# Turned attention probabilities moved to their key partitions through device memory: one store and four loads per unit in place of sixteen transfers inside SBUF

## The reference, cut to what matters

```python
x = x + attn(_layernorm(x))            # 32 query heads, 8 key-value heads, head width 128
# k_full, v_full: 16 gathered blocks of 32 keys, and 128 new keys: 640 keys
scores = einsum('bhld,bhtd->bhlt', qh, k_full) / sqrt(128)
attn = softmax(scores, axis=-1)
out = einsum('bhlt,bhtd->bhld', attn, v_full)
x = x + xattn(_layernorm(x), ctx, mask)
x = x + ffn(_layernorm(x))
```

## Time and profile before

| | us |
|---|---|
| median of 3 runs | 2031.06 (2029.79 to 2032.06) |
| the profiled execution's own time | 2030.36 |
| its span in the profile | 2028.2 |
| first attention: first move of probabilities issued | 44.8 |
| first attention: last key tile through POOL | 964 |
| PE busy | 1908.0, 94% of the span |
| DVE busy | 1357.2, 67% |
| ACT busy | 1029.7, 51% |
| POOL busy | 978.2, 48% |

### The profile page before, as it was taken

How to read it: one execution, slowest core, us unless ns; L and a number is a source line. 1 busy time by engine, 2 the same in 40 slices (tenths; PEclk the granted TensorE clock), 3 DMA queues, 4 the chain that set the end, 5 groups by cost and what they waited for, 6 DMA issues and landing times.

```text
span 2028.2 us, 31742 instructions
## 1 busy us (share of the span) xinstructions
PE 1908.0 (94%) x10146; PEld 1609.7 (79%) x10146; DVE 1357.2 (67%) x2177; ACT 1029.7 (51%) x2265; POOL 978.2 (48%) x771
## 2 busy tenths in 40 slices
PE   8898989889988989888899999999999999999998
PEld 6677777777777777777688888888888888887887
DVE  7677777777777777776766666666666666668132
ACT  3555555555555555555544444444444444446444
POOL 3667676666667666767222222222222222224643
PEclk9999999999999999999899999999999999999999
DMA  7444444444444444455111110111111110103232
GB/s 246 117 117 107 107 111 115 106 110 107 113 110 108 108 109 113 104 135 136 48 45 45 44 44 34 38 44 44 44 44 44 44 41 26 38 8 94 94 115 78
DMA packets 229433, 169.03 MB, mean 83 GB/s; under 512 B 24834, under 2 KB 194946, under 8 KB 228866
## 3 DMA queue, kind: packets, MB, share of 16 engines
q1 hardware_dynamic: 229378, 168.33, 31.0%
HBM read 82.26 MB, written 2.10 MB: 42 GB/s over the span
## 4 chain that ended last, share of the span: by engine, by line
PE 53%; POOL 20%; issue 17%; DVE 5%; ACT 3%; SPq 1%; DMA 0%; POOLq 0%; DVEq 0%; ACTq 0%
PE bank L1304 15%; PE bank L1306 15%; PE bank L1305 15%; POOL pT_lo L454 13%; POOL wq_sin L421 2%; POOL wx_lo L434 2%; POOL wq_rot L418 2%; PE bank L1505 2%; PE bank L1506 1%; PE bank L1550 1%; PE bank L1551 1%; PE bank L1560 1%; DVE probT L962 1%; POOL wo_lo L438 1%; SPq L277 1%
## 5 line engine op out<-in xcount | busy, mean ns | idle before, releaser
L454 POOL TENSOR_TENSOR pT_lo<-pT_lo,pT_hi 128x512 fp32r<-128x512 f32 x320 | 410.0, 1291 | 278.2 <-ACT pT_hi L546 278.2
L973 DVE SCALAR_TENSOR_TENSOR xacc<-bank,rinv,xacc 128x512 f32<-128x512 f32 x504 | 367.8, 741 | 44.1 <-PE bank L1306 44.1
L605 ACT ACTIVATE prob<-bank,negmax 128x640 f32<-128x640 f32 x256 | 203.8, 796 | 345.7 <-DVE negmax L954 343.9
L962 DVE STREAM_TRANSPOSE probT<-prob 128x640 f32<-128x640 f32 x256 | 214.7, 839 | 36.7 <-ACT prob L605 36.7
L954 DVE TENSOR_REDUCE negmax<-bank 128x1 f32<-128x640 f32 x256 | 201.3, 787 | 0.4 <-PE bank L1384 0.4
L438 POOL TENSOR_TENSOR xwo_lo<-xwo_raw,xwo_hi 128x512 fp32r<-128x512 f32 x32 | 41.4, 1293 | 332.0 <-ACT xwo_hi L546 332.0
L1304 PE MATMUL bank<-pT_hi,V_hi 128*128 128x512 f32 x320 | 135.5, 423 | 66.4 <-POOL pT_lo L454 66.3
L546 ACT ACTIVATE pT_hi<-pT_lo 128x512 fp32r<-128x512 f32 x320 | 192.6, 625 | 10.3 <-DMA pT_lo<-probT 9.8
L438 POOL TENSOR_TENSOR xwq_lo<-xwq_raw,xwq_hi 128x512 fp32r<-128x512 f32 x32 | 41.4, 1293 | 283.6 <-ACT xwq_hi L546 283.6
L1304 PEld LDWEIGHTS bank<-pT_hi,V_hi 128*128 128x128 f32 x320 | 59.9, 187 | 115.7 <-POOL pT_lo L454 105.1
L714 ACT ACTIVATE xprob<-xscore,negmax 128x128 f32<-128x128 f32 x256 | 99.4, 391 | 91.5 <-DVE negmax L1126 91.5
(11 more groups left out here) (197 smaller groups left out, 5593.6 us busy)
## 6 DMA issues: line engine op xcount, KB each, us to landing
pT_lo<-probT SPq DMA_DIRECT2D x1024, 80.0 KB, 2.1
w_raw<-in_w SPq DMA_DIRECT2D x64, 256.0 KB, 2.8
wx_raw<-in_wq SPq DMA_DIRECT2D x32, 256.0 KB, 2.7
wo_raw<-in_wo SPq DMA_DIRECT2D x32, 256.0 KB, 2.6
wx_raw<-in_xwv SPq DMA_DIRECT2D x16, 512.0 KB, 3.2
xwk_raw<-in_xwk SPq DMA_DIRECT2D x32, 256.0 KB, 3.4
xwq_raw<-in_xwq SPq DMA_DIRECT2D x32, 256.0 KB, 3.2
xwo_raw<-in_xwo SPq DMA_DIRECT2D x32, 256.0 KB, 2.6
```

The lines of the kernel that those rows point to most:

```text
L454: g.tensor_tensor(pT_lo[:, (u - 1) % 2, j, :], pT_lo[:, (u - 1) % 2, j, :].bitcast(F32), pT_hi[:, j, :], ALU.subtract).then_inc(a["pTlo"], 1)
L605: s.activation(prob[:, i % 2, :].rearrange("p (a t) -> p a t", a=2), S_bank[i % 2], ACT.Exp, bias=negmax[:, u % 2, i:i + 1], scale=1.0, ac ...
L962: v.transpose(probT[:, u % 2, :, i * 32:(i + 1) * 32], prob[:, i % 2, :].rearrange("p (j n) -> p j n", n=32)).then_inc(a["turned"], 1)
L973: v.scalar_tensor_tensor(xacc[:, 4 * half + i, :], M, rinv[:, k, i:i + 1], xacc[:, 4 * half + i, :], ALU.mult, ALU.add).then_inc(sems["y"], 1)
```

## The change

`a_turn` now issues one store of the whole slot of `probT` (128 partitions by 2560 floats, 1.31 MB) to a tensor `turned` in device memory, waits for it, and issues four loads, one for each quarter j of the key partitions. Each load takes from all four quarters i of the stored tensor: 32 partitions, 4 runs of 640 floats, 328 KB. For this the layouts change: `probT` and `pT_lo` have the key quarter or the token quarter ahead of the key tile. ACT, POOL and PE thus read a key tile of `pT_lo` as 4 pieces of 128 floats 640 apart (`key_tile`), and DVE's transpose reads its blocks in another order. DVE's wait before it fills a slot of `probT` again is for the store, no longer for all moves.

```diff
-                pT_lo = sb(lo_, "pT_lo", [P, 2, KT, HALF], F32R)
+                pT_lo = sb(lo_, "pT_lo", [P, 2, 4, KT, P], F32R)
-                probT = sb(lo_, "probT", [P, 2, KB, P])
+                probT = sb(lo_, "probT", [P, 2, 4, KT, P])
+        turned = nc.dram_tensor("turned", (2, P, KB * P), F32).ap()
+        s_st = [sem(f"turned_stored{i}") for i in range(2)]
-        TURN = 16 * 16
+        TURN = 4 * 16
+        def key_tile(slot, j):
+            return pT_lo[:, slot, :, j, :]
+        def four(t):
+            return t.rearrange("p (i n) -> p i n", i=4)
@@ a_turn, SP
-                for i in range(4):
-                    for j in range(4):
-                        from_ = probT[i * 32:(i + 1) * 32, u % 2].rearrange("p (t j) n -> p t j n", j=4)[:, :, j, :]
-                        sp.dma_start(pT_lo[j * 32:(j + 1) * 32, u % 2, :, i * P:(i + 1) * P].bitcast(F32), from_)\
-                          .then_inc(s_pT[u % 2], 16)
+                sp.dma_start(turned[u % 2], probT[:, u % 2].rearrange("p j t n -> p (j t n)")).then_inc(s_st[u % 2], 16)
+                sp.wait_ge(s_st[u % 2], (it * 4 + u // 2 + 1) * 16)
+                for j in range(4):
+                    sp.dma_start(pT_lo[j * 32:(j + 1) * 32, u % 2].rearrange("p i t n -> p i (t n)").bitcast(F32),
+                                 turned[u % 2].rearrange("(i k) (j n) -> k i j n", i=4, j=4)[:, :, j, :])\
+                      .then_inc(s_pT[u % 2], 16)
@@ a_step, POOL
-                        g.tensor_tensor(pT_lo[:, (u - 1) % 2, j, :], pT_lo[:, (u - 1) % 2, j, :].bitcast(F32),
-                                        pT_hi[:, j, :], ALU.subtract).then_inc(a["pTlo"], 1)
+                        tile = key_tile((u - 1) % 2, j)
+                        g.tensor_tensor(tile, tile.bitcast(F32), four(pT_hi[:, j, :]), ALU.subtract).then_inc(a["pTlo"], 1)
@@ prob_hi, ACT
-                    copy(pT_hi[:, j, :], pT_lo[:, (u - 1) % 2, j, :].bitcast(F32)).then_inc(a["pThi"], 1)
+                    copy(four(pT_hi[:, j, :]), key_tile((u - 1) % 2, j).bitcast(F32)).then_inc(a["pThi"], 1)
@@ turn, DVE
-                    dve.wait_ge(s_pT[u % 2], (it * 4 + u // 2) * TURN)
-                v.transpose(probT[:, u % 2, :, i * 32:(i + 1) * 32],
-                            prob[:, i % 2, :].rearrange("p (j n) -> p j n", n=32)).then_inc(a["turned"], 1)
+                    dve.wait_ge(s_st[u % 2], (it * 4 + u // 2) * 16)
+                v.transpose(probT[:, u % 2, :, :, i * 32:(i + 1) * 32],
+                            prob[:, i % 2, :].rearrange("p (t j n) -> p j t n", j=4, n=32)).then_inc(a["turned"], 1)
@@ pv, PE
-                           [pT_hi[:, j, :], pT_lo[:, u % 2, j, :]], j == 0, j == KT - 1)
+                           [pT_hi[:, j, :], key_tile(u % 2, j)], j == 0, j == KT - 1)
```

## The result

The changed kernel took 2036.63 us, median of 6 runs (2033.24 to 2039.18), beside 2030.79 us, median of 6 (2029.79 to 2032.86), for the kernel before in the same series. The ratio is 1.0025, with a 95% interval of 1.0015 to 1.0035: slower by 5.1 us by that ratio, between 3 and 7 (the two medians lie 5.8 us apart). The forecast was 2031.5 us, in a range of 2025 to 2058. The range holds the time, and the likeliest case, within 0.2% of no change, is missed by a little.

What follows compares the result with a forecast made beforehand. The first attention was taken as bound by PE and what feeds it, the move ending almost no wait. Units 0, 59 and 63 together added about 0.5 us to 2030.36, or 2031.6 from the median; predicted 2031.5, range 2025 to 2058.

Steps and rivals of the forecast that it cites:

- the likeliest case: Whole kernel: the saved issues shorten nothing and nothing new is late, so time within 0.2% of no change; chance 0.54.
- the term for unit 59: Unit 59's store queues behind 1.83 MB of loads at 404 GB/s; key tile at 907.8 us, 0.9 us later and exposed.
- The slack of 13.9 and 14.25 us: Odd units behind a K or V copy: time allowed from first issue to ACT's key tile 0 before lateness costs.
- The sum of 12.3 us: Odd unit's move: store 4.6, wait 0.1, loads 7.2 us, plus 0.2 to 0.5 for the `wo` load ahead.
- The fixed part of a store: Store landing: fastest 256 KB store lands in 2.0 us, 0.65 us of it bytes at 404 GB/s, 1.35 us fixed.
- ACT's wait for DMA stays near 10 us in all: Sign that the forecast is right: ACT's total wait for DMA unchanged, 9.8 us in the kernel before.
- The pieces at zero: Key tile work on DVE, POOL and PE in smaller pieces: no added time taken; POOL's upper bound 109 ns.
- SP's queue: Loads behind the move on SP: `wq` reached after 7.3 us, not 10.3; `wo` and the next odd unit unchanged.
- Unit 63: Unit after the long series of unit 62: its move starts up to 1 us earlier, worth 0 to -0.2 us.
- The first rival: ACT's key tile 0 of odd units: two landings outlast the slack; at 14.7 us, +26 us, 2057 us; chance 0.27.

Runs made afterwards that it cites:

- the fourth experiment: The changed kernel with one more 32 KB store, and a wait for it, between each unit's store and its loads: 2057.19 us, ratio 1.0118.

## Why the prediction was right, and where it was not

**The range** holds the measured time, but not for a reason that the prediction gave: it reached up to 2058 for a loss in every odd unit, and no term of its sum or rival of its list was a loss of 5 us in one unit. That it holds 2036.63 us is luck. What was right is the loop, and what was wrong is the term for unit 59.

**The slack of 13.9 and 14.25 us** held, and it is what the forecast stood on. The two kernels with added landings lose by pair of units what their lateness beyond these bounds gives (0.48 against 0.43 us, 1.87 against 1.88, the second in part by luck, as said above). Below the bounds the loop has the length of before, 689.91 us against 690.08.

**The sum of 12.3 us** for an odd unit was 13.2 and 13.5 us, about 1 us more. The windows of the changed kernel, 518 to 528 us, show the store (first two) and the loads:

```profile
518.00:519.00 1.00, 1.00 (x6) 0.78 (x6) 1.00 (x2) 0.00 (x0) 1.00 (x1) 1.00 1.17 492
519.00:520.00 1.00, 1.00 (x6) 0.84 (x5) 0.37 (x1) 0.60 (x1) 0.21 (x1) 1.00 1.06 451
...
524.00:525.00 1.00, 1.00 (x7) 0.91 (x7) 0.70 (x2) 1.00 (x3) 0.00 (x0) 1.00 1.08 225
525.00:526.00 1.00, 0.95 (x5) 0.43 (x3) 1.00 (x2) 0.06 (x1) 0.86 (x1) 1.00 1.05 205
...
527.00:528.00 1.00, 1.00 (x7) 0.91 (x6) 0.19 (x1) 1.00 (x3) 1.00 (x2) 1.00 1.05 210
```

The store was priced at 4.6 us and takes 4.5 without and 5.0 to 5.5 with a `wo` load ahead; its rate is above the 404 GB/s assumed, so more of it is fixed. The loads were priced at 239 GB/s and 7.2 us; they run at 205 to 241, 220 on average, and take 8.1 us. The rate that I took from the V blocks was too high for them.

**The fixed part of a store** was taken as 1.35 us. The 32 KB stores of the fourth experiment let SP go on after 1.5 us.

**"ACT's wait for DMA stays near 10 us in all"** was wrong by its own working. ACT is free 11.5 and 11.7 us after the store (529.81 - 1.66 - 516.63, 558.70 - 1.80 - 545.18), so a move of the 12.3 us that the prediction gives odd units must show 0.8 and 0.6 us of wait in each of some 30 of them, an estimated 20 us, though it is hidden. It was 57.5 us, and DVE's part fell by 43.8. The sign to name was the sum of the two idle times in front of the exponential, 2.5 us before and after.

**The pieces at zero** were right: 1291 ns, 625 ns, and the layouts alone at 0.9993. **SP's queue** was right as well: `wq` is reached 536.37 - 529.84 = 6.5 us after the even unit's store, where 7.3 was said and 10.3 was needed before, and the next odd unit starts 28.55 us after the last, 28.40 before.

**The term for unit 59 failed.** It said +0.9 us and measured +5.4. Its step was the time from the issue of unit 59's store to ACT's key tile, and two parts of it were short. First, the queue: 1.83 MB of loads and the 1.31 MB store were put at 404 GB/s, the rate of stores that alone fill the engines. Those 3.14 MB took from about 892.6 to 904.3 us, an estimated 268 GB/s. The window of the changed kernel, 893 to 897 us, and then that of the kernel before:

```profile
893.00:897.00 4.00, 4.00 (x22) 3.51 (x22) 2.56 (x4) 2.29 (x6) 1.29 (x1) 1.00 0.91 278
```

```profile
893.00:897.00 4.00, 4.00 (x22) 3.47 (x21) 2.56 (x5) 2.30 (x6) 1.60 (x2) 1.00 0.91 273
```

The last row was there to be read before the change: this queue, with these loads, moved 273 GB/s at a share of 0.91. I had taken the rate from another stretch. Second, the loads took 8.3 us and not 7.3. That makes 11.1 - 7.6 = 3.5 and 1.0 us, and 0.9 + 3.5 + 1.0 is the 5.4. (The prediction also put the store's landing only 0.4 us behind its last byte, with no row for it; of the 1.35 us that it called fixed, no run shows how much lies there.)

Behind it stands the mechanism that I did not see in the earlier trace rows. Sixteen small transfers behind 1.83 MB of loads cost a wait of 3.1 us. In the kernel before the first of them landed after 6.5 us, and the last, issued at 904.7 us, after 2.1 us, as each does in the loop: it met no queue any more. What was late is its issue, 11.9 us after the first where it is 9.8 in the loop, and these 2.1 us are what the unit took longer (14.0 us to key tile 0 in place of 11.9). A single large store whose landing is waited for meets all of the queue, and the loads can't even be issued until it is through.

**Unit 63** was to cost 0 to -0.2 us and cost 0.9 us in this execution, with the granted clock at 0.77 in place of 1.00 around it. The sum had no term for a lower clock. The same 0.9 us came with the same fall in the kernel before with two loads moved. In the changed kernel with the light loads the step between the two tiles is 12.31 us as well, with the clock at 1.00 and a wait of 1.06 us for the move. So the cause of this microsecond stays open, and the 5.1 us of the runs don't need it.

**The first rival** (landings longer than the slack, 0.27) is what happened at one place only: it put units 0, 59 and 63 at some 2.5 us each, and unit 59 alone was 5.4 while the odd units of the loop stayed within their slack. With a move 1 us later still they would have begun to count.

## What to carry to other kernels

In this loop a serial chain of two landings stood in for sixteen issues at no cost. It could because the first consumer's next wait ended later than the chain did; read that bound from the timeline, and read the sum of the idle times in front of the next instruction, not one of them. Then look for the few places where something large stands ahead in the same queue: here one large transfer that was waited for paid for the whole queue (11.1 us to land in place of 4.5 in the loop), where many small ones were still being issued while it drained (the last of them landed after 2.1 us, as in the loop), and the rate of that queue has to be read in its own windows. What is saved on a queue that has 1% of the chain is worth nothing, and it was so here in both directions.

## What the runs showed of the hardware

- The issue of a transfer from SBUF to SBUF took 0.63 us on SP with one run of 2560 bytes per partition, and 0.64 us with five of 512.
- A store of 1.31 MB from 128 partitions to device memory landed in 4.5 us, and in 5.1 to 5.5 us behind one 256 KB load; two windows of 1 us in one of these moved 451 and 492 GB/s. The same bytes came back in 5.5 us to 128 partitions at once and in 8.1 us by four loads to 32 partitions each.
- A 32 KB store was waited for and passed in 1.5 us.
- The queue of one 256 KB and three 512 KB loads with what stands behind them moved 273 and 278 GB/s at 893 to 897 us, at a DMA share of 0.91; with contiguous rows in place of rows 16 KB apart it was 279 there, and the store behind landed after 9.2 us in place of 11.1.
- In the changed kernel, and among others in two that lost nothing, the granted clock fell to between 0.66 and 0.86 for 5 to 10 us near 1000 to 1015 us. From the `xwo` load to the second bias load such executions took 48.8 to 49.4 us, the others 46.9 to 47.1. What starts it isn't known. Falls of the same kind at 875 to 880 us (0.77, 0.67, 0.68) went with 0.75 us in that pair of units, in kernels with the change and in one with direct transfers.
